# One Sign instruction over two neighbouring ring tiles instead of one per tile, in a two-layer graph kernel

## The reference, cut to what matters

```python
def _L0(x, adj, W, b):
    x1 = swish((adj @ x) @ W + b)
    return swish((adj @ x1) @ W + b)

def _L1(x, adj, W, b):
    a_hat = adj + eye(8192)
    d = sum(a_hat, axis=1) ** -0.5
    return ((a_hat * d[:, None] * d[None, :]) @ x) @ W.T + b

h = maximum(layernorm(x), 0); x = x + _L0(h, adj, W0, b0)
h = maximum(layernorm(x), 0); x = x + _L1(h, adj, W1, b1)
```

## Time and profile before

| | |
|---|---|
| median of 3 runs | 1545.54 us (1544.24 to 1545.72) |
| the profiled execution, its own time | 1544.59 us |
| its span in the profile | 1542.7 us |
| TensorE matmul busy | 1407.3 us, 91% |
| VectorE busy | 965.9 us, 63% |
| ScalarE busy | 628.0 us, 41%, of which Sign 488.6 us (with the readout of its sum) |
| HBM read | 284.69 MB |

### The profile page before, as it was taken

How to read it: one execution, slowest core, us unless ns; L and a number is a source line. 1 busy time by engine, 2 the same in 40 slices (tenths; PEclk the granted TensorE clock), 3 DMA queues, 4 the chain that set the end, 5 groups by cost and what they waited for, 6 DMA issues and landing times.

```text
span 1542.7 us, 18073 instructions
## 1 busy us (share of the span) xinstructions
PE 1407.3 (91%) x6598; PEld 655.9 (43%) x6598; DVE 965.9 (63%) x2271; ACT 628.0 (41%) x751; POOL 33.6 (2%) x30
## 2 busy tenths in 40 slices
PE   2567989999999999998799888799999999999998
PEld 0223434444444444343344444344444444444444
DVE  5989998999987977584754655677523332332331
ACT  5887887888776767555540111222100000000000
POOL 1100000000000000000000000010000000000000
PEclk9899999999999999999999999999999999999999
DMA  8699999999998997775740111111100000000000
GB/s 302 271 346 402 402 400 397 393 400 405 401 369 363 360 363 294 310 300 213 310 172 28 35 35 41 62 62 42 34 15 21 21 14 21 21 14 21 21 14 22
DMA packets 77164, 297.71 MB, mean 193 GB/s; under 512 B 5648, under 2 KB 38928, under 8 KB 44304
## 3 DMA queue, kind: packets, MB, share of 16 engines
q1 hardware_dynamic: 58304, 284.71, 47.5%
q10 hardware_dynamic: 18768, 11.80, 2.4%
HBM read 284.69 MB, written 11.80 MB: 192 GB/s over the span
## 4 chain that ended last, share of the span: by engine, by line
PE 73%; DVE 11%; DMA 8%; ACT 4%; issue 3%; SPq 0%; POOL 0%; DVEq 0%; ACTq 0%
PE acc_ps L525 19%; PE acc_ps L526 19%; PE acc_ps L468 9%; PE acc_ps L469 9%; DMA ring<-adj 8%; PE early_ps L440 6%; PE early_ps L441 5%; PE z_ps L423 3%; ACT unused L633 3%; DVE marks L762 2%; PE kept_ps L449 2%; PE kept_ps L450 2%; DVE ring L292 1%; ACT node_b L594 1%; DVE count_a L797 1%
## 5 line engine op out<-in xcount | busy, mean ns | idle before, releaser
L633 ACT ACTIVATE unused<-ring 128x2048 uint8<-128x2048 uint32 x256 | 488.6, 1908 | 125.4 <-DMA ring<-adj 114.6
L468 PE MATMUL acc_ps<-marks,node_a 128*128 128x512 fp8e4 x1024 | 394.5, 385 | 74.0 <-DVE node_a L755 48.8
L469 PE MATMUL acc_ps<-marks,node_a 128*128 128x512 fp8e4 x1024 | 394.3, 385 | 1.7 <-issue 1.7
L525 PE MATMUL acc_ps<-ring,node_a 128*128 128x512 fp8e4 x1024 | 388.1, 379 | 0.0
L526 PE MATMUL acc_ps<-ring,node_a 128*128 128x512 fp8e4 x1024 | 388.1, 379 | 0.0
L762 DVE TENSOR_SCALAR marks<-ring 128x2048 uint8<-128x2048 f32 x256 | 314.5, 1229 | 58.8 <-DMA ring<-adj 27.8
L292 DVE TENSOR_SCALAR ring<-bits 128x256 uint32<-128x256 uint32 (+1 forms) x784 | 159.0, 276 | 169.0 <-PE acc_ps L526 168.9
L468 PEld LDWEIGHTS acc_ps<-marks,node_a 128*128 128x128 f16 x1024 | 101.3, 99 | 214.2 <-issue 102.1
L674 ACT ACTIVATE nT<-acc_ps 128x512 f32<-128x512 f32 x16 | 9.6, 597 | 433.9 <-PE acc_ps L526 433.9
L440 PE MATMUL early_ps<-marks,node_b 128*128 128x512 fp8e4 x416 | 160.4, 386 | 18.6 <-ACT stage L610 18.6
L525 PE MATMUL acc_ps<-ring,node_b 128*128 128x512 fp8e4 x416 | 162.0, 389 | 0.0
(11 more groups left out here) (111 smaller groups left out, 952.5 us busy)
## 6 DMA issues: line engine op xcount, KB each, us to landing
ring<-adj SPq DMA_DIRECT2D x256, 1024.0 KB, 7.6
xch<-x SPq DMA_DIRECT2D x16, 256.0 KB, 2.9
xn_scratch<-xnew ACTq DMA_DIRECT2D x16, 256.0 KB, 2.3
xch<-xn_scratch SPq DMA_DIRECT2D x16, 256.0 KB, 2.8
out<-xnew ACTq DMA_DIRECT2D x16, 256.0 KB, 2.3
part_scratch<-stage ACTq DMA_DIRECT2D x13, 256.0 KB, 7.3
marks<-part_scratch SPq DMA_DIRECT2D x13, 256.0 KB, 3.0
b_sb<-b SPq DMA_DIRECT2D x2, 64.0 KB, 6.4
```

Source lines behind the costliest of these rows:

```text
L468: nc.tensor.matmul(acc_ps[c % 2][:, :], hi_of(node_a16, j), byte, start=(j == 0), stop=False)
L469: last = nc.tensor.matmul(acc_ps[c % 2][:, :], lo_of(node_a16, j), byte, start=False, stop=(j == NB - 1))
L525: nc.tensor.matmul(into[:, :], hi_of(node, j), byte.bitcast(E4), start=opens, stop=False)
L633: nc.scalar.activation(unused[:, :], slot(g).bitcast(U32), ACT.Sign, accum_out=nz_count[:, g:g + 1]).then_inc(counted, 1)
```

## The change

Sign is left out at even i and covers tiles g-1 and g at odd i, 4096 elements per partition, with one sum for the two. `counted` now counts pairs: SyncE waits, for tile g, for the pair that holds tile g-4. `unused` doubles; `deg` shares `var`'s memory to make room for it; `nz_count` has half as many columns.

```diff
-        unused = sb("unused", [P, TILE], U8)
+        unused = sb("unused", [P, 2 * TILE], U8)
...
-        deg = sb("deg", [P, NB])
+        deg = var
...
-        nz_count = sb("nz_count", [P, NC * TC])
+        nz_count = sb("nz_count", [P, NC * TC // 2])
...
                 sp.wait_ge(marked, g - RING + 1)
-                sp.wait_ge(counted, g - RING + 1)
+                sp.wait_ge(counted, (g - RING) // 2 + 1)
                 load_tile(g)
...
                     act.wait_ge(tile_in[g % RING], 16 * (g // RING + 1))
-                    if g > 0:
-                        act.wait_ge(counted, g)
-                    nc.scalar.activation(unused[:, :], slot(g).bitcast(U32), ACT.Sign,
-                                         accum_out=nz_count[:, g:g + 1]).then_inc(counted, 1)
+                    if i % 2 == 1:
+                        if g > 1:
+                            act.wait_ge(counted, g // 2)
+                        both = ring[:, (g - 1) % RING * TILE:((g - 1) % RING + 2) * TILE]
+                        nc.scalar.activation(unused[:, :], both.bitcast(U32), ACT.Sign,
+                                             accum_out=nz_count[:, g // 2:g // 2 + 1]).then_inc(counted, 1)
                     if c >= 1 and i == SUMS_OUT_AFTER:
                         sums_out(c - 1)
...
-                dve.wait_ge(counted, NC * TC)
+                dve.wait_ge(counted, NC * TC // 2)
...
-                link(nc.vector.tensor_reduce(nz_chunk[:, :], nz_count[:, :].rearrange("p (c i) -> p c i", i=TC), AX.X, ALU.add))
+                link(nc.vector.tensor_reduce(nz_chunk[:, :], nz_count[:, :].rearrange("p (c i) -> p c i", i=TC // 2), AX.X, ALU.add))
```

## The result

The changed kernel takes 1589.75 us (median of 4 runs, 1585.25 to 1596.61) against 1545.63 us for the kernel before (4 runs, 1544.24 to 1549.18). The ratio is 1.0286, 95% interval 1.0263 to 1.0308: slower by 44 us. The forecast was slower by 27, with 1573 in a range of 1554 to 1594.

What follows compares the result with a forecast made beforehand. Tile supply was taken to pace chunks 1 to 5 and TensorE the later ones; B 18.2, A 4 and D 5.1 sum to 27.3 us, added to 1545.5 for about 1573 us, range 1554 to 1594.

Steps and rivals of the forecast that it cites:

- Length of the Sign: ScalarE's Sign over 4096 elements: 3.62 us, 3.72 with the readout, against 4.02 for two separate ones.
- Term A: Chunk 0, up to the first projection: later first Signs and loads add 4 us, between 2 and 6.
- Term B: Ring with pairs: half-ring turn 11.0 us, 45.5 us per chunk; chunks 1 to 5 +13.8, with next three +18.2 us.
- disturbances: Tile supply in chunks 1 to 5: 2.9 us per chunk beyond undisturbed spacing, 42.7 seen against 39.8.
- The next three chunks: Chunks after the first five paced ones: go to 45.5 us where shorter, +3.0, +1.4 and 0.
- The tenth chunk: Within the stretch from 450 to 550 us, where everything was to take as long as before.
- Term D: Early sums of chunks 12 to 15: longer TensorE waits and a clock loss, +5.1 us, between 2 and 8.
- Chunk 12's clock loss: TensorE after chunk 12's wait grows to 3.2 us: half of four us of matmuls, +2 us.
- Marks costed at nothing: VectorE's marks, which loads also wait for: no cost, as VectorE had 17.7 us to spare in 213.7.
- rival 1: Ring supply barely suffers: a pair lands in 6.9 us or less, B is 0, total 1555 us; chance 0.12.
- Rival 2: Marks and meeting transfers stretch the ring's turn to 12.5 us, a chunk to 50, total 1612; chance 0.08.
- rivals 3 and 4: Ring: 3, paired loads land together, 1541 us, chance 0.03; 4, turn near 10.2 to 10.6, no change, chance 0.02.

Runs made afterwards that it cites:

- `early_out` first: Changed kernel, but early_out of chunks 9 to 14 done at tile 0 of the next chunk, ahead of the pair's Sign and sums_out: 1556.02 us, ratio 1.0066.

## Why the prediction was right or wrong

**Right in direction, place and range, wrong in the price of supply.** The chance of 0.95 for slower rested on "a slot is free only when its neighbour has landed too", and that is what the runs show. Predicted +27.3, measured +43.5 between the two spans. That this stayed inside the range is in part luck: the sum for supply came near only because the change's Sign is long, and the range had no place for the tenth chunk's 8.5 us.

- *Length of the Sign:* 3.62 predicted, 3.615 measured.
- *Term A:* +4 predicted, +4.6 measured. One part of it was not seen: the activation table, loaded at 0.74 us before, is now loaded behind the first wait. Before, then now:

```profile
0.74 1.28 ACT L633 ACT_TABLE_LOAD   x1 [0.74 <-PEq L1155]
```

```profile
18.60 1.28 ACT L635 ACT_TABLE_LOAD   x1 [18.60 <-DMA ring<-adj]
```

- *Term B, the five chunks:* +13.8 predicted, +17.0 measured. The turn was 0.6 us too short, mostly since the second load's issue (0.42 us after the first) was costed at nothing. The more important failure is the step's form: "One turn of a half is: both loads issued, second tile landed, Sign, next issue", with a fixed load. The load is not fixed. It came out near the sum only because the change's Sign is long; with a Sign of 1.9 us the measured parts, 7.43 + 2.01 + 0.48, give 9.92 us and 39.7 per chunk, and the runs show 45.7 and 46.9. The 2.9 us of "disturbances" per chunk with its middle taken hid this.
- *The next three chunks:* +4.4 predicted, +11.2 measured. This is the worst mis-sized of the terms that had a price. "Go to 45.5 where they are shorter" takes the slower of supply and TensorE. The rows show 49.2, 46.7 and 47.8 with TensorE waiting in between (43.57, 44.47 and 46.29 us busy): where both are nearly equal, each now waits for the other at times, and the waits add to the time. Most of it is the ring: against 132.5 us before, the same three chunks take 139.0 with pairs and no Sign at all, 139.6 with single Signs and paired release, and 143.7, 140.0 and 141.5 in the three kernels with the change's Signs. What the long Sign adds to the 6.5 to 7 of the ring is not clear of the differences between profiles.
- *The tenth chunk:* 0 predicted, +8.5 measured. "From 450 to 550 us ... everything as long as before" was wrong. `early_out` stands there at tile 1, and I had read the early sums only where they already waited. With `early_out` first, all of it went. Its size differs between profiles: with the table loaded early the wait was 2.53 us and the chunk 4.3 longer than before.
- *Term D:* +5.1 predicted, +2.2 measured. The waits were right to 0.1 us. Chunk 12's clock loss of 2 us did not come: after 3.27 us of waiting the clock stood at 1.00, after 3.28 in chunk 13 at the 1.2 GHz level for most of four us. Before, chunk 13 had stood at that level for the whole six us that were looked at the earlier trace rows, so it even gained.

```profile
626.20:629.20 3.00, 2.98 (x14) 1.38 (x15) 1.27 (x3) 2.64 (x1) 0.00 (x0) 1.00 0.78 279
682.40:686.40 4.00, 3.96 (x11) 1.46 (x12) 0.19 (x1) 3.64 (x2) 0.00 (x0) 0.58 0.79 296
```

- *Marks costed at nothing:* right for the change. SyncE's waits from 107 to 338 us (total, times, longest):

```profile
SPq L332 <- ACT unused L635: 186.8, 39, 7.1
SPq L317 <- DVE marks L764: 9.8, 21, 2.0
```

- *Rivals:* rival 1 fell; it needed a pair landed in 6.9 us or less. In the turn shown above it landed 7.9 us after the first load's issue (0.48 + 7.43), over chunks 1 to 5 in 7.5 in the median and never under 7.1. By the fit of the Trainium skill's page "DMA: Bandwidth & Descriptors", section "Anatomy of one DMA — SWDGE (gpsimd) path", which is for another issuing path, it would have been an estimated 6.8; the measurement decides. Rival 2's marks and rivals 3 and 4 did not come.

**The rule on grouping.** The page "Perfetto Trace Analysis", section "Optimizing Scalar/DVE Operations", of the Trainium skill also says that where ScalarE is not saturated but causes bubbles elsewhere, breaking instructions up may let work complete sooner. The trace agrees in the direction: larger instructions, 37 us less of ScalarE time, 44 us more of the whole. But two short Signs at the odd tile cost as much (1594 us), so for supply it is the release that costs, not the length of the instruction.

**What stays open.** Why a load takes longer when its slot is released sooner, so that two pairs never get under 45.7 us per chunk. The trace shows where the time goes: over chunks 1 to 5 a pair's second tile lands 2.6 to 2.7 us after its first in every paired kernel, about as before, but the next pair's first tile 3.1 to 3.4 us after that, against 2.7 before. A wait for the slowest of the DMA engines could look like this; that is a guess, as no run here shows the engines apart. Five slots were not tried: `deg` had to share its memory to make 2 KB per partition free, and one more tile needs 8.

## What to carry to other kernels

Before merging an operation over several buffers of a ring, count what is released together: two pairs of slots supplied hardly more than three single slots (45.7 to 47.4 against 47.0 to 48.0 us per chunk), with a long Sign, a short one and none. Price a ring in a DMA-paced stretch by the number of transfers that its release rule lets queue behind the awaited one, as measured on a ring of that kind, not by a sum with a fixed load time. And look along the order of an engine that runs ahead for short copies that another engine needs at once: moving one such copy per chunk ahead of its neighbours was worth 26 us here.

## What the runs showed of the hardware

- With one-megabyte loads, four slots released one by one moved 399 to 401 GB/s in chunks 1 to 5; two pairs or three single slots moved 355 to 369, with a Sign of 0, 1.9 or 3.6 us. I had expected a shorter release to show in full.
- Where the first activation waits for one tile its table load ran ahead of the wait, at 0.74 us; where it waits for two tiles (four kernels here) the load stood behind the first wait, at 18.5 to 18.8 us, and its 1.28 us became visible.
- Two waits of TensorE of nearly the same length, 3.27 and 3.28 us, left the clock at 1.00 once and at 0.58 (mean of four us) once.
